# A fused attention block: a quarter's own maximum, its bias on ScalarE, fades once a stage, the division on GpSimd

## The chip, the cores and the metric

The kernel runs on one core of a Trainium2 chip. The metric is the device time of one execution in microseconds; the numbers shown are medians of several runs. A profile is one execution, recorded by the hardware profiler. The engines are called PE (TensorE), DVE (VectorE), ACT (ScalarE), POOL (GpSimd) and SP (SyncE). They run their own instruction streams in order and wait for each other by semaphores.

## The reference

The inputs are x (8 x 128 x 512) and a context (8 x 2048 x 384). Three blocks follow each other, each on a layer-normalised x and each added to it:

```python
# 1: cross attention, 8 heads of 64, every token of x against 2048 context rows
q = norm(x) @ Wq;  k = ctx @ Wk;  v = ctx @ Wv
x = x + softmax(q k^T / 8) v @ Wo + bo
# 2: causal attention in x, softmax over the query axis, divided by sqrt(512)
# 3: feed-forward 512 -> 2048 -> 512 with relu; hidden and weights rounded to fp8, the result to fp16
```

All time that matters here is in block 1. Products of float32 numbers are made in three passes over float16 halves (high x high, high x low, low x high), so each operand is split into a rounded copy (`_h`) and a remainder (`_l`).

## The kernel before, in words

A batch element b has four pairs of heads p; b and p together make a stage n (32 stages). Each stage has four quarters q of 512 context rows; a quarter of a stage is a slot s (128 slots). In slot s the engines work on different quarters at once:

- PE (`steady`, L478): `value_tiles(s)` fills v_ps with a share of v, `key_quarter(s)` fills k_ps with the keys of quarter s, `weighted_values(s - 5)` multiplies transposed probabilities by v into o_ps, `scores(s - 1)` makes the scores of the quarter before into e_ps (two buffers). v_ps and k_ps have one buffer each, so PE waits in slot s + 1 until DVE has made the low halves (`v_split`, L370; `k_split`, L387).
- ACT (L766): `v_high(s)` copies v_ps to float16; then for quarter x = s - 2 `fade_of(x)` (L712, not where q = 0) and `exps(x, 0)`: the exponential of the first head as float16 (p_h, L726) and again as float32 (p_f, L728); `k_high(s)` (L705); `exps(x, 1)` for the second head. Once a stage (q = 1) `ctx_high` rounds a quarter of the next context (L691), and once it starts a load.
- DVE (L994): `running_maximum(s - 2)` (L917), `accumulate(s - 6)` (L936), `v_low(s)` (L904), after the last quarter of a stage `o_norm` (L950), then `k_low(s)` (L911). In the last 16 slots a `split_weight` (L961) for the later blocks comes behind each slot.
- POOL (L1217): `p_low(s - 2)` takes p_h from p_f, giving the low half of the probabilities (L1205), and once a stage `ctx_low` does so for the context (L1197).
- SP (L317): transposes p_h and p_l by DMA.

The softmax is computed while the quarters go by. `running_maximum` reduces e_ps (with the sign turned, so it is a minimum that is kept), takes the minimum with the floor of the quarter before (L927), and makes the bias of the exponential from the new floor (L930). Where q > 0 it also takes the step from the old to the new floor (L933), from which ACT makes a fade factor; `accumulate` multiplies what has been summed by the fade and adds o_ps (L946). Where q = 0 there is no old floor, and acc is a copy (L941). `fade_of(x)` also waits for `acc_ready`, that is for the accumulate which DVE has in its stream behind the maximum of the same slot. `o_norm` takes the reciprocal of the sum of probabilities (a column of ones in v makes it), adds the two halves of the output and multiplies (L953 to L958).

The order of all streams is written out by hand; there is no planner. After slot 127 a drain of seven steps mixes the last quarters with the output projection (L596 to L600 on PE, L828 on ACT, L1106 on DVE, L1241 on POOL). At its start ACT waits for the last split weight and issues eight loads of x (L825 to L827). The second attention and the feed-forward follow. In it ACT alternates Identity with a bias (`q_or_k`, L806) with Exp (`prob_exp`, L813).

Of the kernel before, what the change touches and what calls it, by code (L numbers as in the profile page):

```python
# [4 lines left out]
F32 = mybir.dt.float32  # L5
# [20 lines left out]
VW = 2 * DH + 2  # L26
# [4 lines left out]
EXP_SCALE = DH ** -0.5 / (W_SCALE * W_SCALE)  # L31
SHIFT = 4.0
# [3 lines left out]
SLOTS = B * PAIRS * QUARTERS  # L36
# [19 lines left out]
def perceiver_kernel(nc, x, ctx_t, xwq, xwk, xwv, xwo, xbo, awq, abq, awk, abk, awv, abv,  # L56
# [9 lines left out]
        ("q_max", [P, 2, 1], F32), ("floor", [P, 2, 2, 1], F32), ("bias", [P, 2, 2, 1], F32), ("step", [P, 2, 2, 1], F32),  # L66
        ("fade", [P, 4, 2, 1], F32), ("acc", [P, 2, VW], F32), ("o_rec", [P, 2, 1], F32), ("o_sum", [P, 2, DH], F32),
# [52 lines left out]
    assert ffn2_end <= ctx1_base  # L120

    (o_all, ident, causal, bo_row, bv_row, b2_row, bq_col, bk_col, b1_col, b2_half, stats, mean_var, rstd, exponent,
     q_max, floor, bias, step, fade, acc, o_rec, o_sum) = keep.values()
# [22 lines left out]
    with ExitStack() as ctx:  # L146
# [48 lines left out]
        k_split = sem("k_split")  # L195
        e_filled = sem("e_filled")
        e_maxed = sem("e_maxed")
        floor_ready = sem("floor_ready")
        bias_ready = sem("bias_ready")
        step_ready = sem("step_ready")  # L200
        fade_ready = sem("fade_ready")
        p_hi = sem("p_hi")
        p_full = sem("p_full")
# [48 lines left out]
        out_stored = sem("out_stored")  # L252

        block = ctx.enter_context(nc.Block())

# [400 lines left out]
        def _(act):  # L656
# [55 lines left out]
            def fade_of(s):  # L712

                act.wait_ge(step_ready, s // QUARTERS * 3 + s % QUARTERS)
                if s >= QUARTERS:
                    act.wait_ge(acc_ready, s - 3)
                act.activation(fade[:, s % 4, :, :], step[:, s % 2, :, :], ACT.Exp, scale=EXP_SCALE).then_inc(fade_ready, 1)  # L717

            def exps(s, h):

                act.wait_ge(bias_ready, s + 1)
# [4 lines left out]
                act.activation(p_h[:, s % H_RING, h, :], e_ps[s % 2][:, h, :], ACT.Exp, scale=EXP_SCALE,  # L726
                               bias=bias[:, s % 2, h, :]).then_inc(p_hi, 1)
                act.activation(p_f[:, s % F_RING, h, :], e_ps[s % 2][:, h, :], ACT.Exp, scale=EXP_SCALE,  # L728
                               bias=bias[:, s % 2, h, :]).then_inc(p_full, 1)

            wq_high(0)
            wq_high(1)
# [32 lines left out]

            def steady(s):  # L766
                x = s - X_LAG
                if s < SLOTS:
                    v_high(s)
                if 0 <= x < SLOTS:  # L770
                    if x % QUARTERS:
                        fade_of(x)
                    exps(x, 0)
                if s < SLOTS:
                    k_high(s)
                if 0 <= x < SLOTS:
                    exps(x, 1)

            for s in range(SLOTS):
                n, q = stage_of(s)  # L780
# [81 lines left out]
        def _(dve):  # L862
# [54 lines left out]
            def running_maximum(s):  # L917

                q = s % QUARTERS
                dve.wait_ge(e_filled, s + 1)  # L920
                if q == 0:
                    dve.tensor_reduce(floor[:, s % 2, :, :], e_ps[s % 2][:, :, :], AX, ALU.max, negate=True)\  # L922
                        .then_inc(floor_ready, 1)
                else:
                    dve.tensor_reduce(q_max[:, :, :], e_ps[s % 2][:, :, :], AX, ALU.max, negate=True).then_inc(e_maxed, 1)  # L925
                    dve.wait_ge(e_maxed, s // QUARTERS * 3 + q)
                    dve.tensor_tensor(floor[:, s % 2, :, :], q_max[:, :, :], floor[:, (s - 1) % 2, :, :], ALU.min)\  # L927
                        .then_inc(floor_ready, 1)
                dve.wait_ge(floor_ready, s + 1)
                dve.tensor_scalar(bias[:, s % 2, :, :], floor[:, s % 2, :, :], EXP_SCALE, SHIFT, ALU.mult, ALU.add)\  # L930
                    .then_inc(bias_ready, 1)
                if q:
                    dve.tensor_tensor(step[:, s % 2, :, :], floor[:, s % 2, :, :], floor[:, (s - 1) % 2, :, :], ALU.subtract)\  # L933
                        .then_inc(step_ready, 1)

            def accumulate(s):  # L936

                q = s % QUARTERS
                dve.wait_ge(pv_done, s + 1)
                if q == 0:  # L940
                    ins = dve.tensor_copy(acc[:, :, :], o_ps[s % 2][:, 0:2 * VW].rearrange("p (h d) -> p h d", h=2))  # L941
                else:
                    dve.wait_ge(fade_ready, s // QUARTERS * 3 + q)
                    dve.wait_ge(acc_ready, s)
                    for h in range(2):
                        ins = dve.scalar_tensor_tensor(acc[:, h, :], acc[:, h, :], fade[:, s % 4, h, :],  # L946
                                                       o_ps[s % 2][:, h * VW:h * VW + VW], ALU.mult, ALU.add)
                ins.then_inc(acc_ready, 1)

            def o_norm(n):  # L950
                b, p = pair_of(n)
                dve.wait_ge(acc_ready, 4 * n + 4)
                dve.reciprocal(o_rec[:, :, :], acc[:, :, DH:DH + 1]).then_inc(o_rec_ready, 1)  # L953
                dve.tensor_tensor(o_sum[:, :, :], acc[:, :, 0:DH], acc[:, :, DH + 1:2 * DH + 1], ALU.add)\
                    .then_inc(o_sum_ready, 1)
                dve.wait_ge(o_rec_ready, n + 1)
                dve.wait_ge(o_sum_ready, n + 1)
                dve.tensor_tensor(o_all[:, b, p * P:p * P + P].rearrange("p (h d) -> p h d", h=2), o_sum[:, :, :],  # L958
                                  o_rec[:, :, :].broadcast_to([P, 2, DH]), ALU.mult).then_inc(o_ready, 1)

            def split_weight(i):  # L961
                k = weight_slot(i)
# [31 lines left out]
            def steady(s):  # L994

                done = s - PV_LAG - 1
                if 0 <= s - X_LAG < SLOTS:
                    running_maximum(s - X_LAG)
                if 0 <= done < SLOTS:
                    accumulate(done)  # L1000
                if s < SLOTS:
                    v_low(s)
                if 0 <= done < SLOTS and done % QUARTERS == 3:
                    o_norm(done // QUARTERS)
                if s < SLOTS:
                    k_low(s)

# [162 lines left out]
        def _(pool):  # L1170
# [46 lines left out]
            for s in range(SLOTS):  # L1217
                n, q = stage_of(s)
                if s >= X_LAG:
                    p_low(s - X_LAG)  # L1220
                if s < 2:
# [19 lines left out]
            for s in range(SLOTS, SLOTS + 6):  # L1241
                if s - X_LAG < SLOTS:
                    p_low(s - X_LAG)
                add_bias(s - SLOTS)
                if s > SLOTS + 1:
                    inverse_deviation(s - SLOTS - 2)
# [41 lines left out]
```

## Time and profile before

| | us |
|---|---|
| median of 3 runs | 1053.88 (1052.25 to 1054.06) |
| the profiled execution | 1052.84 |
| its span, first to last instruction | 1051.0 |
| PE busy | 971.7 (92%) |
| DVE busy | 755.9 (72%) |
| ACT busy | 558.6 (53%) |
| POOL busy | 418.1 (40%) |

The loop of 128 slots fills the span from about 50 to about 808 us; ahead of it x is normalised and q is made, behind it come the drain, the second attention and the feed-forward. A row of a timeline gives start, duration, engine, line, operation, the tile written and the tiles read, how many such instructions, and in brackets how long the engine was idle before and who released it. A duration begins when the engine takes up the instruction and ends with its last write, so neighbours on one engine can overlap a little, and an instruction that is held on its way is simply long. PE's ends are modelled, so starts are the safer numbers there.

### The profile page before, as it was taken

How to read it: one execution, taken by the hardware profiler on the slowest of the kernel's cores; microseconds unless marked ns; L12 is line 12 of the kernel's file. 1: busy time of each engine (PE TensorE's matmuls, PEld its weight loads, DVE VectorE, ACT ScalarE, POOL GpSimd, SP SyncE). 2: the span in 40 equal slices, each digit the busy share in tenths (PEclk: the TensorE clock that was granted, in tenths of full speed). 3: DMA queues.
4: the chain of work that ended last, by engine and by line, in shares of the span. 5: the costliest groups of instructions: out<-in, count | busy, mean ns of one | idle time of the engine just before them, and what ended most of it. 6: DMA issues, size and time to landing. Idle time of an engine off the chain costs nothing.

```text
span 1051.0 us, 19633 instructions
## 1 busy us (share of the span) xinstructions
PE 971.7 (92%) x7469; PEld 577.6 (55%) x7472; DVE 755.9 (72%) x1344; ACT 558.6 (53%) x1007; POOL 418.1 (40%) x227
## 2 busy tenths in 40 slices
PE   4889999999999999999999999999887889999998
PEld 2456656665565656565555666565554444554443
DVE  6467787878778787878788778778877763574533
ACT  3366666666666666666666666665554321222220
POOL 3155455545444455545454455444333650110000
PEclk9899999999999999999999999999999899999999
DMA  7146665667657666678656666668565701003302
GB/s 270 61 131 121 121 122 121 121 122 145 123 116 121 120 121 121 121 127 140 126 120 120 117 121 123 121 105 152 122 126 117 130 1 41 1 31 90 91 31 80
DMA packets 295789, 115.86 MB, mean 110 GB/s; under 512 B 272529, under 2 KB 272529, under 8 KB 295697
## 3 DMA queue, kind: packets, MB, share of 16 engines
q1 hardware_dynamic: 281264, 86.82, 46.0%
q10 hardware_dynamic: 14432, 27.79, 8.8%
q8 instruction: 61, 1.00, 0.4%
q14 instruction: 32, 0.25, 0.1%
HBM read 45.36 MB, written 2.10 MB: 45 GB/s over the span
## 4 chain that ended last, share of the span: by engine, by line
DVE 51%; PE 21%; ACT 16%; issue 8%; ACTq 2%; DMA 1%; POOL 1%; SPq 0%; POOLq 0%; DVEq 0%
PE e_ps L362 14%; DVE floor L927 13%; DVE q_max L925 10%; DVE k_l L915 8%; ACT p_f L728 7%; ACT k_h L710 6%; DVE bias L930 5%; DVE acc L946 5%; DVE floor L922 3%; PE o_ps L593 3%; DVE step L933 1%; PE v_ps L362 1%; ACT p_h L726 1%; PE k_ps L362 1%; ACTq L755 1%
## 5 line engine op out<-in xcount | busy, mean ns | idle before, releaser
L1205 POOL TENSOR_TENSOR p_l<-p_f,p_h 128x1024 f16<-128x1024 f32 x128 | 279.0, 2180 | 395.5 <-ACT p_f L728 387.8
L915 DVE TENSOR_TENSOR k_l<-k_ps,k_h 128x512 f16<-128x512 f32 x128 | 88.5, 692 | 142.1 <-ACT k_h L710 142.1
L726 ACT ACTIVATE p_h<-e_ps,bias 128x512 f16<-128x512 f32 x256 | 177.2, 692 | 20.0 <-DVE bias L930 19.8
L728 ACT ACTIVATE p_f<-e_ps,bias 128x512 f32<-128x512 f32 x256 | 177.5, 694 | 0.0
L362 PE MATMUL v_ps<-wv_h,ctx_h 128*128 128x256 f16 x768 | 125.7, 272 | 44.2 <-DVE v L907 38.9
L717 ACT ACTIVATE fade<-step 128x2 f32<-128x2 f32 x96 | 19.5, 203 | 241.4 <-DVE acc L946 232.9
L927 DVE TENSOR_TENSOR floor<-q_max,floor 128x2 f32<-128x2 f32 x96 | 134.1, 1397 | 3.3
L362 PEld LDWEIGHTS v_ps<-wv_h,ctx_h 128*128 128x128 f16 x768 | 66.3, 97 | 109.3 <-issue 101.2
L362 PE MATMUL v_ps<-wv_l,ctx_h 128*128 128x256 f16 x768 | 126.0, 273 | 0.0
L362 PE MATMUL v_ps<-wv_h,ctx_l 128*128 128x256 f16 x768 | 126.0, 273 | 0.0
L925 DVE TENSOR_REDUCE q_max<-e_ps 128x2 f32<-128x1024 f32 x96 | 116.6, 1215 | 0.0
L1197 POOL TENSOR_TENSOR ctx_l<-raw,ctx_h 128x1536 f16<-128x1536 f32 x32 | 99.3, 3104 | 29.1 <-ACT ctx_h L691 29.1
L423 PE MATMUL o_ps<-v,pt_h 128*128 128x130 f16 x1024 | 106.2, 220 | 3.0 <-DVE acc L946 1.6
L362 PE MATMUL k_ps<-ctx_h,wk_h 128*128 128x512 f16 x384 | 104.2, 380 | 0.5 <-DVE k_l L915 0.5
L362 PE MATMUL k_ps<-ctx_h,wk_l 128*128 128x512 f16 x384 | 103.9, 379 | 0.0
L362 PE MATMUL k_ps<-ctx_l,wk_h 128*128 128x512 f16 x384 | 103.8, 379 | 0.0
L426 PE MATMUL o_ps<-v,pt_l 128*128 128x65 f16 x1024 | 102.7, 192 | 0.0
L423 PEld LDWEIGHTS o_ps<-v,pt_h 128*128 128x128 f16 x1024 | 91.8, 97 | 19.3 <-issue 4.6
L426 PEld LDWEIGHTS o_ps<-v,pt_l 128*128 128x128 f16 x1024 | 90.4, 98 | 14.6
L907 DVE TENSOR_TENSOR v<-v_ps,v 128x512 f16<-128x512 f32 x128 | 87.5, 684 | 6.8 <-ACT v L702 6.8
L702 ACT ACTIVATE v<-v_ps 128x512 f16<-128x512 f32 x128 | 78.9, 616 | 15.0 <-PE v_ps L362 14.8
L362 PEld LDWEIGHTS v_ps<-wv_l,ctx_h 128*128 128x128 f16 x768 | 75.3, 98 | 8.9
(153 smaller groups left out, 1404.8 us busy)
## 6 DMA issues: line engine op xcount, KB each, us to landing
raw<-in_ctx_t ACTq DMA_DIRECT2D x26, 768.0 KB, 4.8
w_raw<-in_w_t SPq DMA_DIRECT2D x32, 256.0 KB, 2.8
raw<-in_ctx_t SPq DMA_DIRECT2D x6, 768.0 KB, 4.6
pt_h<-p_h SPq DMA_TRANSPOSE x128, 3.5
pt_l<-p_l SPq DMA_TRANSPOSE x128, 3.1
xr<-in_x ACTq DMA_DIRECT2D x8, 256.0 KB, 5.2
out<-xr SPq DMA_DIRECT2D x8, 256.0 KB, 2.0
x_in<-in_x SPq DMA_DIRECT2D x4, 256.0 KB, 5.1
```

The costliest lines, as they stand in the source:

```text
L362: mm = pe.matmul(acc, a(c), m(c), start=(i == 0), stop=(i == len(todo) - 1))
L423: pe.matmul(acc_bank[:, h * VW:h * VW + VW], pt_h[:, s % T_RING, h * JT + j, :], v[g][:, tile, 2 * (p % 2) + h, :], start=(j == 0 and h == ...
L426: mm = pe.matmul(acc_bank[:, h * VW:h * VW + DH + 1], pt_l[:, s % T_RING, h * JT + j, :], v[g][:, tile, 2 * (p % 2) + h, 0:DH + 1], start= ...
L702: act.activation(v[g][:, j0:j0 + 2, :, 0:DH], v_ps[:, :].rearrange("p (j h d) -> p j h d", j=2, d=DH), ACT.Copy).then_inc(v_hi, 1)
L726: act.activation(p_h[:, s % H_RING, h, :], e_ps[s % 2][:, h, :], ACT.Exp, scale=EXP_SCALE, bias=bias[:, s % 2, h, :]).then_inc(p_hi, 1)
L728: act.activation(p_f[:, s % F_RING, h, :], e_ps[s % 2][:, h, :], ACT.Exp, scale=EXP_SCALE, bias=bias[:, s % 2, h, :]).then_inc(p_full, 1)
L907: dve.tensor_tensor(v[g][:, j0:j0 + 2, :, DH + 1:2 * DH + 1], v_ps[:, :].rearrange("p (j h d) -> p j h d", j=2, d=DH), v[g][:, j0:j0 + 2, ...
L915: dve.tensor_tensor(k_l[:, n % 2, cols], k_ps[:, :], k_h[:, n % 2, cols], ALU.subtract).then_inc(k_split, 1)
L925: dve.tensor_reduce(q_max[:, :, :], e_ps[s % 2][:, :, :], AX, ALU.max, negate=True).then_inc(e_maxed, 1)
L927: dve.tensor_tensor(floor[:, s % 2, :, :], q_max[:, :, :], floor[:, (s - 1) % 2, :, :], ALU.min)\
L1197: pool.tensor_tensor(ctx_l[b % 2][:, q, :, :], raw[:, i % 2, :, :], ctx_h[b % 2][:, q, :, :], ALU.subtract).then_inc(ctx_split, 1)
L1205: pool.tensor_tensor(p_l[:, s % L_RING, :, :], p_f[:, s % F_RING, :, :], p_h[:, s % H_RING, :, :], ALU.subtract).then_inc(p_split, 1)
```

## The change

- DVE keeps only the reduction in each quarter (`quarter_maximum`); there is no running floor. Its result q_max has two buffers.
- ACT makes the bias of the quarter, from the quarter's own maximum (`quarter_bias`, an Identity with scale and bias), as its first work in a slot, ahead of `v_high(s)`.
- When a stage has all its four biases, DVE takes their minimum (`stage_low`, behind `v_low` in the slot of its last maximum), and ACT makes four fades for each of the two heads in two operations (`fade_of(n)`, behind the last exponentials of the stage).
- `accumulate` multiplies each quarter's o_ps by that quarter's fade and adds what is there, two operations in every quarter; acc has two buffers, one for a stage.
- `o_norm` moves to POOL, behind `p_low`, but for its reciprocal, which DVE does behind the accumulate (`o_reciprocal`). It also stands in POOL's drain, ahead of `add_bias`.

```diff
+            def quarter_bias(s):
+                n, q = stage_of(s)
+                act.wait_ge(e_maxed, s + 1)
+                act.activation(bias[:, n % 2, :, q], q_max[:, s % 2, :], ACT.Identity, scale=EXP_SCALE, bias=SHIFT)\
+                    .then_inc(bias_ready, 1)
+            def fade_of(n):
+                act.wait_ge(low_ready, n + 1)
+                if n >= 2:
+                    act.wait_ge(acc_ready, 4 * n - 4)
+                for h in range(2):
+                    ins = act.activation(fade[:, n % 2, h, :], bias[:, n % 2, h, :], ACT.Exp, scale=-1.0, bias=low[:, n % 2, h, :])
+                ins.then_inc(fade_ready, 1)
...
             def steady(s):
                 x = s - X_LAG
+                if 0 <= x < SLOTS:
+                    quarter_bias(x)
                 if s < SLOTS:
                     v_high(s)
                 if 0 <= x < SLOTS:
-                    if x % QUARTERS:
-                        fade_of(x)
                     exps(x, 0)
                 if s < SLOTS:
                     k_high(s)
                 if 0 <= x < SLOTS:
                     exps(x, 1)
+                    if x % QUARTERS == 3:
+                        fade_of(x // QUARTERS)
...
+            def quarter_maximum(s):
+                dve.wait_ge(e_filled, s + 1)
+                dve.tensor_reduce(q_max[:, s % 2, :], e_ps[s % 2][:, :, :], AX, ALU.max, negate=True).then_inc(e_maxed, 1)
+            def stage_low(n):
+                dve.wait_ge(bias_ready, 4 * n + 4)
+                dve.tensor_reduce(low[:, n % 2, :, :], bias[:, n % 2, :, :], AX, ALU.min).then_inc(low_ready, 1)
             def accumulate(s):
...
                 dve.wait_ge(pv_done, s + 1)
                 if q == 0:
-                    ins = dve.tensor_copy(acc[:, :, :], o_ps[s % 2][:, 0:2 * VW].rearrange("p (h d) -> p h d", h=2))
+                    dve.wait_ge(fade_ready, n + 1)
+                    if n >= 2:
+                        dve.wait_ge(o_ready, n - 1)
...
+                for h in range(2):
+                    new, total, faded = o_ps[s % 2][:, h * VW:h * VW + VW], acc[:, n % 2, h, :], fade[:, n % 2, h, q:q + 1]
+                    if q == 0:
+                        ins = dve.tensor_scalar(total, new, faded, None, ALU.mult)
+                    else:
+                        ins = dve.scalar_tensor_tensor(total, new, faded, total, ALU.mult, ALU.add)
                 ins.then_inc(acc_ready, 1)
-            def o_norm(n):
+            def o_reciprocal(n):
                 dve.wait_ge(acc_ready, 4 * n + 4)
+                if n:
+                    dve.wait_ge(o_ready, n)
+                dve.reciprocal(o_rec[:, :, :], acc[:, n % 2, :, DH:DH + 1]).then_inc(o_rec_ready, 1)
...
+            def o_norm(n):
+                b, p = pair_of(n)
+                pool.wait_ge(o_rec_ready, n + 1)
+                pool.tensor_tensor(o_sum[:, :, :], acc[:, n % 2, :, 0:DH], acc[:, n % 2, :, DH + 1:2 * DH + 1], ALU.add)\
+                    .then_inc(o_sum_ready, 1)
+                pool.wait_ge(o_sum_ready, n + 1)
+                pool.tensor_tensor(o_all[:, b, p * P:p * P + P].rearrange("p (h d) -> p h d", h=2), o_sum[:, :, :],
+                                   o_rec[:, :, :].broadcast_to([P, 2, DH]), ALU.mult).then_inc(o_ready, 1)
```

## Rows read from the trace of the kernel before

**Rows 1.** The page of the profile, its first line.
```profile
span 1051.0 us, 19633 instructions
```

**Rows 2.** Busy time by stretch: PE, PEld, DVE, ACT, POOL, clock, DMA.
```profile
300.00:400.00 100.00, 95.37 (x837) 60.06 (x833) 80.00 (x137) 64.96 (x119) 50.61 (x22) 1.00 0.68 122
...
950.00:1000.00 50.00, 50.00 (x234) 22.66 (x232) 27.49 (x63) 13.39 (x20) 0.00 (x0) 1.00 0.30 90
```

**Rows 3.** Waits, 200 to 700 us: total us, times, longest.
```profile
ACT fade L717 <- DVE acc L946: 156.4, 63, 2.9
...
PE v_ps L362 <- DVE v L907: 21.1, 43, 0.6
```

**Rows 4.** Timeline of one slot with q > 0.
```profile
400.67 0.60 ACT L710 ACTIVATE k_h<-k_ps 128x512 f16<-128x512 f32 x1
...
401.30 0.69 DVE L915 TENSOR_TENSOR k_l<-k_ps,k_h 128x512 f16<-128x512 f32 x1 [1.39 <-ACT k_h L710]
...
401.91 1.21 DVE L925 TENSOR_REDUCE q_max<-e_ps 128x2 f32<-128x1024 f32 x1
...
402.50 2.13 POOL L1205 TENSOR_TENSOR p_l<-p_f,p_h 128x1024 f16<-128x1024 f32 x1 [3.99 <-ACT p_f L728]
...
403.16 1.49 DVE L927 TENSOR_TENSOR floor<-q_max,floor 128x2 f32<-128x2 f32 x1
...
404.83 0.61 DVE L946 SCALAR_TENSOR_TENSOR acc<-acc,fade,o_ps 128x130 f32<-128x130 f32 x2
...
405.35 0.69 DVE L907 TENSOR_TENSOR v<-v_ps,v 128x512 f16<-128x512 f32 x1
405.53 0.20 ACT L717 ACTIVATE fade<-step 128x2 f32<-128x2 f32 x1 [2.62 <-DVE acc L946]
405.64 0.69 ACT L726 ACTIVATE p_h<-e_ps,bias 128x512 f16<-128x512 f32 x1
...
406.18 0.49 PE L362 MATMUL v_ps<-wv_h,ctx_h 128*128 128x256 f16 x3 [0.49 <-DVE v L907]
```

**Rows 5.** Timeline of a slot with q = 0, POOL and DVE.
```profile
414.75 2.14 POOL L1205 TENSOR_TENSOR p_l<-p_f,p_h 128x1024 f16<-128x1024 f32 x1 [3.99 <-ACT p_f L728]
416.84 3.10 POOL L1197 TENSOR_TENSOR ctx_l<-raw,ctx_h 128x1536 f16<-128x1536 f32 x1
...
415.40 1.50 DVE L930 TENSOR_SCALAR bias<-floor 128x2 f32<-128x2 f32 x1
...
417.16 0.68 DVE L907 TENSOR_TENSOR v<-v_ps,v 128x512 f16<-128x512 f32 x1
```

**Rows 6.** Timeline of PE: v of slots 6, 8 and 127, k of slot 6.
```profile
82.86 0.50 PE L362 MATMUL v_ps<-wv_h,ctx_h 128*128 128x256 f16 x3
...
84.83 0.81 PE L362 MATMUL k_ps<-ctx_h,wk_h 128*128 128x512 f16 x3
...
93.78 0.50 PE L362 MATMUL v_ps<-wv_h,ctx_h 128*128 128x256 f16 x3
...
800.55 0.49 PE L362 MATMUL v_ps<-wv_h,ctx_h 128*128 128x256 f16 x3 [0.45 <-DVE v L907]
```

**Rows 7.** Groups of instructions: busy us, mean ns, then idle before.
```profile
L691 ACT ACTIVATE ctx_h<-raw 128x1536 f16<-128x1536 f32 x32 | 48.1, 1503 | 3.9 <-DMA raw<-in_ctx_t 3.9
...
L662 ACT ACT_TABLE_LOAD x1 | 1.3, 1283 | 2.6 <-issue 2.6
...
L1228 POOL TENSOR_TENSOR xr<-xr,bo_row 128x512 f32<-128x512 f32 x8 | 10.2, 1280 | 0.0
```

**Rows 8.** Timeline at the end of the loop.
```profile
807.83 0.69 DVE L915 TENSOR_TENSOR k_l<-k_ps,k_h 128x512 f16<-128x512 f32 x1 [1.39 <-ACT k_h L710]
...
808.43 0.42 DVE L966 TENSOR_SCALAR av_h<-raw 128x512 f16<-128x512 f32 x1
...
809.61 4.41 ACTq L827 DMA_DIRECT2D xr<-in_x  x8
```

More of the change, by code:

```diff
@@ L65, in perceiver_kernel @@
         ("stats", [P, B, 6], F32), ("mean_var", [P, B, 2], F32), ("rstd", [P, B], F32), ("exponent", [P, B], F32),
-        ("q_max", [P, 2, 1], F32), ("floor", [P, 2, 2, 1], F32), ("bias", [P, 2, 2, 1], F32), ("step", [P, 2, 2, 1], F32),
-        ("fade", [P, 4, 2, 1], F32), ("acc", [P, 2, VW], F32), ("o_rec", [P, 2, 1], F32), ("o_sum", [P, 2, DH], F32),
+        ("q_max", [P, 2, 2], F32), ("bias", [P, 2, 2, QUARTERS], F32), ("low", [P, 2, 2, 1], F32),
+        ("fade", [P, 2, 2, QUARTERS], F32), ("acc", [P, 2, 2, VW], F32), ("o_rec", [P, 2, 1], F32), ("o_sum", [P, 2, DH], F32),
     ])
@@ L122, in perceiver_kernel @@
     (o_all, ident, causal, bo_row, bv_row, b2_row, bq_col, bk_col, b1_col, b2_half, stats, mean_var, rstd, exponent,
-     q_max, floor, bias, step, fade, acc, o_rec, o_sum) = keep.values()
+     q_max, bias, low, fade, acc, o_rec, o_sum) = keep.values()
     q_h, q_l = queries.values()
@@ L197, in perceiver_kernel @@
         e_maxed = sem("e_maxed")
-        floor_ready = sem("floor_ready")
         bias_ready = sem("bias_ready")
-        step_ready = sem("step_ready")
+        low_ready = sem("low_ready")
         fade_ready = sem("fade_ready")
@@ L710, in k_high @@
                 act.activation(k_h[:, n % 2, q * QW:q * QW + QW], k_ps[:, :], ACT.Copy).then_inc(k_hi, 1)
[L712 to L717, printed above, removed]
+            def quarter_bias(s):
[10 more added lines that the diff above has]
+                ins.then_inc(fade_ready, 1)
             def exps(s, h):
+                n, q = stage_of(s)
                 act.wait_ge(bias_ready, s + 1)
@@ L726, in exps @@
                 act.activation(p_h[:, s % H_RING, h, :], e_ps[s % 2][:, h, :], ACT.Exp, scale=EXP_SCALE,
-                               bias=bias[:, s % 2, h, :]).then_inc(p_hi, 1)
+                               bias=bias[:, n % 2, h, q:q + 1]).then_inc(p_hi, 1)
                 act.activation(p_f[:, s % F_RING, h, :], e_ps[s % 2][:, h, :], ACT.Exp, scale=EXP_SCALE,
-                               bias=bias[:, s % 2, h, :]).then_inc(p_full, 1)
+                               bias=bias[:, n % 2, h, q:q + 1]).then_inc(p_full, 1)
             wq_high(0)
@@ L915, in k_low @@
                 dve.tensor_tensor(k_l[:, n % 2, cols], k_ps[:, :], k_h[:, n % 2, cols], ALU.subtract).then_inc(k_split, 1)
-            def running_maximum(s):
-                q = s % QUARTERS
+            def quarter_maximum(s):
                 dve.wait_ge(e_filled, s + 1)
[L921 to L934, printed above, removed]
@@ L942, in accumulate @@
                 else:
-                    dve.wait_ge(fade_ready, s // QUARTERS * 3 + q)
                     dve.wait_ge(acc_ready, s)
-                    for h in range(2):
-                        ins = dve.scalar_tensor_tensor(acc[:, h, :], acc[:, h, :], fade[:, s % 4, h, :],
-                                                       o_ps[s % 2][:, h * VW:h * VW + VW], ALU.mult, ALU.add)
+                for h in range(2):
[4 more added lines that the diff above has]
+                        ins = dve.scalar_tensor_tensor(total, new, faded, total, ALU.mult, ALU.add)
@@ L948, in accumulate @@
                 ins.then_inc(acc_ready, 1)
-            def o_norm(n):
-                b, p = pair_of(n)
+            def o_reciprocal(n):
                 dve.wait_ge(acc_ready, 4 * n + 4)
[L953 to L959, printed above, removed]
+                if n:
+                    dve.wait_ge(o_ready, n)
+                dve.reciprocal(o_rec[:, :, :], acc[:, n % 2, :, DH:DH + 1]).then_inc(o_rec_ready, 1)
@@ L997, in steady @@
                 if 0 <= s - X_LAG < SLOTS:
-                    running_maximum(s - X_LAG)
+                    quarter_maximum(s - X_LAG)
                 if 0 <= done < SLOTS:
                     accumulate(done)
+                    if done % QUARTERS == 3:
+                        o_reciprocal(done // QUARTERS)
                 if s < SLOTS:
                     v_low(s)
-                if 0 <= done < SLOTS and done % QUARTERS == 3:
-                    o_norm(done // QUARTERS)
+                if 0 <= s - X_LAG < SLOTS and (s - X_LAG) % QUARTERS == 3:
+                    stage_low((s - X_LAG) // QUARTERS)
                 if s < SLOTS:
@@ L1220, in _ @@
                     p_low(s - X_LAG)
+                done = s - PV_LAG - 1
+                if done >= 0 and done % QUARTERS == 3:
+                    o_norm(done // QUARTERS)
                 if s < 2:
@@ L1243, in _ @@
                     p_low(s - X_LAG)
+                done = s - PV_LAG - 1
+                if done % QUARTERS == 3:
+                    o_norm(done // QUARTERS)
                 add_bias(s - SLOTS)
```

2 lines of the change are left out of this document (1 added, 1 removed).

## The prediction

> **What bounds the kernel now.** I read the busy shares by stretch first, then the waits of the long middle stretch, then the timeline of one slot (a slot is one step s of the steady loop: one quarter of the keys for one pair of heads), and last the start and the end of the loop.
>
> The profiled execution took 1052.84 us, its span is 1051.0 us [rows 1], so 1.84 us lie around it; the median of the runs is 1053.88 us, 1.0 more than this execution. In the middle PE is busy 95.4 of 100 us at a granted clock of 1.00, DVE 80.0, ACT 65.0 [rows 2]. That looks like a kernel bound by TensorE with little to gain. The waits say otherwise: PE waits for the low half of v (DVE L907), ACT's fade waits for DVE's accumulate (156.4 us in 63 waits) [rows 3], and POOL waits for ACT's exponentials (3.99 us ahead of 402.50 [rows 4]). Three engines that wait for each other in turn are a loop, and the timeline shows it [rows 4]. Beginning at the fade (405.53), with the same places of the slot before read 6.12 us earlier where only that slot is shown: 0.11 us to the first exponential (405.64); 1.15 us of two exponentials, to k_h at 400.67 + 6.12 = 406.79; k_h and the other two exponentials until POOL can start p_l, 1.83 (400.67 to 402.50); then p_l, 2.13, at whose end (404.63) the DVE's little floor operation ends too (403.16 + 1.49 = 404.65); 0.2 to the accumulate (404.83) with bias and step between; 0.7 from there to the fade (405.53). The sum is 6.12 us, and that is the period.
>
> The striking row is the floor operation, 1.49 us for 2 elements a partition. It has no work for that: it ends with POOL's operation. The slots with q = 0 show the same with another operation: there the bias (415.40, 1.50 us) ends at 416.90 and POOL's p_l at 414.75 + 2.14 = 416.89, while a v_l with an input in PSUM runs its usual 0.68 us inside POOL's ctx_l [rows 5]. So small DVE operations that touch SBUF alone are held until POOL is done, and those with an operand in PSUM are not. The Trainium skill, "GPSIMD Engine Reference", Specifications, states that the engine shares its SBUF interfaces with VectorE and contends with a DVE instruction in a two-port mode or with two SBUF inputs. By that rule the floor and bias operations are held and the reduction from PSUM is not; the trace agrees (1.49 and 1.50 us against 1.25 us from one reduction to the next operation).
>
> What would TensorE need alone? At the start of the loop there are slots in which it never waits: v begins at 82.86 and at 93.78, two slots later, so 5.46 us a slot with all four of its jobs in it [rows 6]. From 93.78 (slot 8) to 800.55 (slot 127) there are 119 slots in 706.77 us, 5.94 each [rows 6]. The difference, 0.48 us a slot, is what can be had.
>
> **The change part by part.**
>
> *Floor, bias and step leave DVE.* In each slot DVE now has the reduction, the accumulate, v_l and k_l. What goes is 403.16 to 404.83 = 1.67 us a slot [rows 4], and what goes with it is the hold by POOL and therefore the loop. What is late next? I lay out the new slot from the start of v on PE, 0. v is filled at 2.0 (82.86 to 84.83 [rows 6]) and k, with as many columns, at 4.0. The scores of the quarter before were finished just ahead of 0, so the reduction runs 0.15 to 1.4 (401.91 to 403.16 [rows 4]), the accumulate to 2.0. ACT's bias starts at 1.4 and costs 0.11 (below); v_h then waits for PE only, 2.1 to 2.7; v_l to 3.4. PE needs v_l at 5.46: 2 us to spare. The first two exponentials end at 3.9, k_h starts at 4.1, k_l runs 4.7 to 5.4, and PE needs it at 5.46 + 2.0 = 7.5. The other two exponentials end at 5.9, p_l on POOL at 8.0, far ahead of its use. So in this layout PE is last everywhere.
>
> The loops that remain do not hold it either. The tightest goes k_h, k_l, reduction, bias, v_h, two exponentials, k_h: 0.63 + 0.61 + 1.25 + 0.11 + 0.6 (v_h taken like k_h) + 1.16 = 4.36 us [rows 4]. In one slot of four ACT also has the context's high half, 1.5 us [rows 7], and the two fades, between the exponentials and the next bias; that loop is on ACT alone, and in k_h, two exponentials, fades, ctx_h, bias, v_h, two exponentials it is 1.6 (k_h and two exponentials, from the 1.83 above less the hop to POOL) + 0.2 + 1.5 + 0.11 + 0.6 + 1.16 = 5.2 us, still under 5.46. In the last 16 slots DVE splits a weight between k_l and the reduction, about 1.1 us (808.43 to ACT's release near 809.5 [rows 8]); that loop is 5.45, even with PE. I give these slots 0 to 0.1 more, 0 to 1.6 us in all, and take 0.5.
>
> *The bias on ACT.* One operation a slot, 128 x 2, ahead of v_h. The nearest row is the fade, of the same size on the same engine, which holds the next instruction back by 0.11 us (405.53 to 405.64 [rows 4]). It takes the fade's place in three slots of four. Its wait is new: behind it on ACT stand v_h and the exponentials, and PE waits for v_h's sequel. By the layout the wait ends 0.6 us before v_h could start. Cost: between 0 and 0.11 x 128 = 14 us, if it were on the path; I take 0 in the loop because of those 0.6 us and 0.1 at the start of the loop, where ACT is the late one.
>
> *Fades once a stage.* Two ACT operations and one DVE reduction over 4 elements a stage against three and no reduction. Both ACT operations stand after the exponentials, ahead of the accumulate that wants them by some 0.7 us. If DVE's reduction of low is held by POOL it costs at most 2.13 us x 32, of which v_l's 2 us of room takes all but 0.1; I take 0.
>
> *The accumulate.* Twice 128 x 130 from PSUM in every quarter where q = 0 had one copy; 0.1 us more in one slot of four, hidden. Could POOL now hold the accumulate, since it comes at once after the reduction and has acc in SBUF? Below, it isn't held; above, it starts at p_l's end at about 2.5, and v_l at 3.1 still has its room. Cost 0 by both.
>
> *The division on GpSimd.* A reciprocal stays on DVE; two 128 x 128 operations go to POOL. Between 0 and 1.28 us each, the time of POOL's 128 x 512 [rows 7]; I take 0.4 each. POOL's stage is then 4 x 2.13 + 3.10 + 0.8 = 12.4 of 21.8 us, 14.2 by the upper bound. Behind it in POOL's queue are ctx_l, wanted many slots later, and p_l, wanted two slots later: hidden, 0.
>
> *The sum.* 119 slots x 0.48 = 57.0 us. The end of the loop: v of slot 127 starts at 800.55, its k_l at 807.83, that is 7.3 later; the last split frees ACT's loads at 809.61, 9.1 later [rows 6, 8]. In the new order k_l starts at about 4.7 and the loads go out at about 6.6 with the 16-slot loop's lag: 2.4 us gained. Behind that the drain keeps its waits; the last quarter's bias no longer stands behind two accumulates, and GpSimd has the last division, so between -1 and +2 us, taken as 0.5 gained. Added: 0.1 at the start and 0.5 in the last 16 slots. 1051.0 - 57.0 - 2.4 - 0.5 + 0.6 = 991.7; with 1.84 around it 993.5, and a median 1.0 above: 994.5, say 994. Everything before slot 8 and after the drain stays.
>
> **The rivals.**
>
> *A new loop at ScalarE.* The bias now stands ahead of v_h, and it waits for a reduction; ACT's slot with the context and fades is 5.2 already. If lags that I do not see lengthen the loops to 5.65, the gain falls by 0.19 x 119 = 23 us, to 1017. For: three engines again wait in turn, and the 16-slot loop has no room. Against: 1.1 us of room in the usual slot. Its time: 1005 to 1030.
>
> *It does not do what it says.* The hold passes to another DVE operation or PE finds another wait, and the period stays 5.94: 1053. For: the accumulate touches SBUF. Against: ACT no longer waits for anything behind the accumulate but the fades of a stage, and slots 6 and 7 ran at 5.46 already.
>
> *Slower: ScalarE changes tables.* Identity stands between Exp and Copy in every slot. If each change loaded a table, at 1.28 us [rows 7], twice a slot, the 4.36 loop becomes 6.9 and the kernel 119 x (6.9 - 5.94) = 114 us slower, 1168. It decides from 1.6 us a slot on. Against: the whole trace has one load [rows 7], though Identity (L806) and Exp (L813) already alternate in the second attention. The Trainium skill, "ScalarE: Activation LUTs", Table sets: the hidden batching unit, has the cheap functions, identity among them, in every set; by that rule no load is added, and the single load in the trace agrees. The page prices a switch at 2.66 us with its drain; as an estimate from that, two a slot would make the loss 119 x (4.36 + 5.32 - 5.94) = 445 us.
>
> Would a denser PE be granted less clock? At 950 to 1000 us it is busy 50 of 50 us at 1.00 [rows 2]; I leave this in the slower share.
>
> **How the numbers follow.** Forecast 0.75, with its own range 985 to 1005 (5.40 to 5.55 us a slot, 7 us down and 11 up). ScalarE loop 0.15. No change 0.03, within 0.2%, which is about what a measurement of this kernel can tell. Slower 0.04, and 0.03 for a gain of which most is lost, 1030 to 1050. Faster is then 0.93, same 0.03, slower 0.04. For eight in ten the range is 985 to 1016: most of the forecast's side and the lower half of the ScalarE loop's.
>
> **What would show it.** v on PE every 5.46 us, PE over 99% busy in the middle, no DVE operation of 2 elements above 0.2 us in most slots, ACT's bias ended by the reduction and not ending PE's waits, POOL's division under 1 us a stage. Wrong would be: a period above 5.6, a PE wait for v_l or k_l in the middle, more than one table load, a granted clock under 1.00.

## The result and the profile after

The changed kernel takes 993.21 us (median of 4 runs, 992.35 to 994.40) against 1053.93 beside it: a ratio of 0.9428, 95% interval 0.9412 to 0.9444. The forecast was 994 in a range of 985 to 1016. The span of the profiled execution went from 1051.0 to 991.6 us, 59.4 less.

The page of the changed kernel: the span, then busy time and share of the engines.

```profile
span 991.6 us, 19444 instructions
PE 952.3 (96%) x7472; PEld 582.3 (59%) x7472; DVE 570.1 (57%) x1024; ACT 588.8 (59%) x1103; POOL 440.7 (44%) x291
```

DVE has lost 186 us of busy time, POOL and ACT have gained 23 and 30, and PE does the same work in fewer microseconds. The stretches that answer to [rows 2], in the same columns:

```profile
300.00:400.00 100.00, 100.00 (x900) 65.33 (x897) 58.69 (x100) 75.81 (x144) 57.55 (x34) 1.00 0.65 129
94.00:710.00 616.00, 616.00 (x5528) 403.14 (x5527) 366.35 (x637) 458.75 (x872) 342.73 (x195) 1.00 0.67 135
```

PE is busy 616 of 616 us at a granted clock of 1.00. The waits from 200 to 700 us (total, times, longest) answer to [rows 3]:

```profile
POOL p_l L1209 <- ACT p_f L738: 215.2, 69, 3.3
...
DVE v L919 <- ACT v L702: 78.5, 90, 1.0
ACT bias L716 <- DVE q_max L932: 72.1, 70, 1.8
...
ACT v L702 <- PE v_ps L362: 37.9, 63, 0.6
ACT k_h L710 <- PE k_ps L362: 16.4, 86, 0.2
```

No line of the list is a wait of PE for DVE any more. Every engine waits for another, and the last in each chain is PE: v_h and k_h begin when PE has filled their bank. Read with the timeline of a slot with its bias at 400.51, against [rows 4]:

```profile
399.26 1.23 DVE L932 TENSOR_REDUCE q_max<-e_ps 128x2 f32<-128x1024 f32 x1
399.63 2.13 POOL L1209 TENSOR_TENSOR p_l<-p_f,p_h 128x1024 f16<-128x1024 f32 x1 [2.82 <-ACT p_f L738]
...
400.40 0.60 DVE L954 SCALAR_TENSOR_TENSOR acc<-o_ps,fade,acc 128x130 f32<-128x130 f32 x2
...
400.51 0.20 ACT L716 ACTIVATE bias<-q_max 128x2 f32<-128x2 f32 x1 [0.96 <-DVE q_max L932]
...
401.32 0.60 ACT L702 ACTIVATE v<-v_ps 128x512 f16<-128x512 f32 x1 [0.60 <-PE v_ps L362]
...
401.95 0.69 DVE L919 TENSOR_TENSOR v<-v_ps,v 128x512 f16<-128x512 f32 x1 [0.95 <-ACT v L702]
...
403.26 0.60 ACT L710 ACTIVATE k_h<-k_ps 128x512 f16<-128x512 f32 x1 [0.19 <-PE k_ps L362]
...
403.89 0.69 DVE L927 TENSOR_TENSOR k_l<-k_ps,k_h 128x512 f16<-128x512 f32 x1 [1.25 <-ACT k_h L710]
...
404.61 0.50 PE L362 MATMUL v_ps<-wv_h,ctx_h 128*128 128x256 f16 x3
...
405.09 2.13 POOL L1209 TENSOR_TENSOR p_l<-p_f,p_h 128x1024 f16<-128x1024 f32 x1 [3.34 <-ACT p_f L738]
...
406.50 0.17 DVE L961 RECIPROCAL o_rec<-acc 128x2 f32<-128x2 f32 x1
...
410.07 0.50 PE L362 MATMUL v_ps<-wv_h,ctx_h 128*128 128x256 f16 x3
410.18 1.22 DVE L932 TENSOR_REDUCE q_max<-e_ps 128x2 f32<-128x1024 f32 x1
410.36 0.49 ACT L725 ACTIVATE fade<-bias,low 128x4 f32<-128x4 f32 x2
...
411.32 0.60 DVE L952 TENSOR_SCALAR acc<-o_ps,fade 128x130 f32<-128x130 f32 x2
```

POOL runs p_l over the reduction as before, and now over the accumulate too, and neither is held: the accumulate starts 1.14 us behind the reduction's start, while p_l is still under way. v_l ends at 402.64, and PE wants it at 404.61, so it has the 2 us of room that the layout gave it. v starts on PE every 5.46 us. Slots 8 and 127 on PE, as in [rows 6]:

```profile
93.20 0.50 PE L362 MATMUL v_ps<-wv_h,ctx_h 128*128 128x256 f16 x3
...
743.34 0.50 PE L362 MATMUL v_ps<-wv_h,ctx_h 128*128 128x256 f16 x3
```

That is 650.14 us for 119 slots, 5.463 each.

### The profile page after: what moved, and what is told of

Same layout as the page of the kernel before. It is cut to its first block, busy times and chain, and to the rows that moved or that the text cites. A ratio compares the mean times of both kernels' runs of the same rounds, so it can differ in the third digit from the quotient of the medians.

```text
span 991.6 us, 19444 instructions
## 1 busy us (share of the span) xinstructions
PE 952.3 (96%) x7472; PEld 582.3 (59%) x7472; DVE 570.1 (57%) x1024; ACT 588.8 (59%) x1103; POOL 440.7 (44%) x291
## 4 chain that ended last, share of the span: by engine, by line
PE 89%; DVE 4%; POOL 2%; DMA 1%; ACT 1%; issue 1%; ACTq 0%; SPq 0%; POOLq 0%; DVEq 0%
PE v_ps L362 27%; PE k_ps L362 25%; PE e_ps L362 14%; PE e_ps L403 9%; PE o_ps L423 6%; PE o_ps L426 3%; PE o_ps L593 3%; DMA wq_raw<-in_xwq 1%; PE v_ps L566 1%; DVE stats L1028 0%; DVE x_in L886 0%; ACTq L839 0%; DMA raw<-in_ctx_t 0%; PE k_ps L514 0%; POOL rstd L1191 0%
## 5 line engine op out<-in xcount | busy, mean ns | idle before, releaser
L736 ACT ACTIVATE p_h<-e_ps,bias 128x512 f16<-128x512 f32 x256 | 174.4, 681 | 0.1
L932 DVE TENSOR_REDUCE q_max<-e_ps 128x2 f32<-128x1024 f32 x128 | 156.5, 1223 | 14.4
L702 ACT ACTIVATE v<-v_ps 128x512 f16<-128x512 f32 x128 | 76.2, 595 | 51.8 <-PE v_ps L362 51.5
L716 ACT ACTIVATE bias<-q_max 128x2 f32<-128x2 f32 x128 | 26.3, 205 | 112.6 <-DVE q_max L932 107.0
L710 ACT ACTIVATE k_h<-k_ps 128x512 f16<-128x512 f32 x128 | 76.4, 597 | 24.7 <-PE k_ps L362 23.6
```

What stands on the lines that cost most here:

```text
L932: dve.tensor_reduce(q_max[:, s % 2, :], e_ps[s % 2][:, :, :], AX, ALU.max, negate=True).then_inc(e_maxed, 1)
```

## Where the 59.4 us are

Each figure is a stretch of before less the same stretch of after, so the sum is the difference of the spans.

| stretch | before | after | gained | forecast |
|---|---|---|---|---|
| start to v of slot 8 | 93.78 | 93.20 | 0.6 | -0.1 |
| v of slot 8 to v of slot 127 | 706.77 | 650.14 | 56.6 | 56.5 |
| v of slot 127 to ACT's loads of x | 9.06 | 6.52 | 2.5 | 2.4 |
| the loads to the end | 241.39 | 241.74 | -0.3 | 0.5 |

The start's 0.6 can't be put down to the change: executions of one kernel differ by as much there. In a second trace of the changed kernel, taken later, v of slot 8 starts at 93.86 and not at 93.20. The last row differs too: it is 239.3 us in that second trace, a gain of 2.1 and not a loss of 0.3. The two rows of the loop are the same in both traces to 0.01 us.

## The experiments

Two questions were open though the number was right. Is the loop of four engines the cause, or just that DVE has less to do? And which of the change's parts earn the gain? The twelve runs came in three groups; each is compared with the kernel before on its own chip, at 1052.5 to 1053.9. A gain of 2 or 3 us over the changed kernel is given as a difference of medians, and but for the third group the changed kernel was not run beside them; by the ratios these gains are 0.5 to 0.8 us smaller.

**One line moved in the kernel before.** ACT makes the fade behind the first two exponentials.

```diff
                 if 0 <= x < SLOTS:
-                    if x % QUARTERS:
-                        fade_of(x)
                     exps(x, 0)
+                    if x % QUARTERS:
+                        fade_of(x)
```

> The kernel before with one thing moved: ACT makes the fade behind the first two exponentials of a quarter and not ahead of them, so the exponentials no longer stand behind DVE's accumulate. All of DVE's work and POOL's hold stay. Theory of the loop (fade, exponentials, p_l on POOL, held floor operation, accumulate, fade = 6.12 us): accumulate leaves the loop, which is then 1.15 + 1.83 + 2.13 + 0.15 = 5.3 us, under PE's 5.46, so most of the gain comes: 995 to 1002, with 16 slower slots at the end where a weight is split. Rival, that DVE's amount of work or the small operations themselves are what costs: DVE does exactly what it did, so 1050 to 1054.

Measured: 998.34 us, ratio 0.9487 (0.9471 to 0.9503). All of DVE's and POOL's work is the same, and 55 of the 61 us are gained. The timeline of one slot in the order of time, DVE and ACT, and two PE rows from the last 16 slots:

```profile
400.34 1.26 DVE L927 TENSOR_TENSOR floor<-q_max,floor 128x2 f32<-128x2 f32 x1
401.64 0.17 DVE L930 TENSOR_SCALAR bias<-floor 128x2 f32<-128x2 f32 x1
...
401.79 0.60 DVE L946 SCALAR_TENSOR_TENSOR acc<-acc,fade,o_ps 128x130 f32<-128x130 f32 x2
```
```profile
401.84 0.69 ACT L726 ACTIVATE p_h<-e_ps,bias 128x512 f16<-128x512 f32 x1
...
403.00 0.20 ACT L717 ACTIVATE fade<-step 128x2 f32<-128x2 f32 x1
```
```profile
735.00 0.49 PE L362 MATMUL v_ps<-wv_h,ctx_h 128*128 128x256 f16 x3 [0.35 <-DVE v L907]
...
740.88 0.49 PE L362 MATMUL v_ps<-wv_h,ctx_h 128*128 128x256 f16 x3 [0.35 <-DVE v L907]
```

The floor operation is still held, 1.26 us, but the exponentials begin at 401.84, together with the accumulate and not behind it. In the middle PE's period is 5.46 us. What is missing against the changed kernel is at the end of the loop, where the loop with a split weight is longer than PE's: v at 735.00 and 740.88, 5.88 apart.

**The other half of the loop: no hold.** The kernel before, with the fade where it was, and POOL's p_l made to wait for DVE's small operations of the next quarter.

```diff
                 pool.wait_ge(p_hi, 2 * s + 2)
+                after = s + 1
+                if after < SLOTS:
+                    if after % QUARTERS:
+                        pool.wait_ge(step_ready, after // QUARTERS * 3 + after % QUARTERS)
+                    else:
+                        pool.wait_ge(bias_ready, after + 1)
```

> The kernel before with one wait added on POOL: p_l of a quarter starts only when DVE has made the step (where q = 0, the bias) of the next quarter, so POOL is idle when DVE does its small operations and can hold none. All of DVE's work and the fade behind the accumulate stay as before. Theory: the hold is the other half of the loop; without it floor, bias and step take 0.3 us together and the loop k_h, k_l, reduction, small operations, accumulate, fade, two exponentials is 4.8 us, under 5.46: floor near 0.15 to 0.2 us, 994 to 1000 in all. Rival, that the first small operation behind a reduction is slow whatever POOL does: 1050 and above, since POOL now starts even later.

Measured: 996.50 us, ratio 0.9457 (0.9444 to 0.9470). A wait was added and nothing taken away, and the kernel is 5.4% faster. One slot, DVE and POOL:

```profile
399.37 1.23 DVE L925 TENSOR_REDUCE q_max<-e_ps 128x2 f32<-128x1024 f32 x1
400.63 0.16 DVE L927 TENSOR_TENSOR floor<-q_max,floor 128x2 f32<-128x2 f32 x1
```
```profile
401.29 2.13 POOL L1211 TENSOR_TENSOR p_l<-p_f,p_h 128x1024 f16<-128x1024 f32 x1 [3.34 <-DVE step L933]
```

The same floor operation, first behind the same reduction, takes 0.16 us when POOL is idle and 1.49 when it is not. So both halves are shown: to open the loop at either place is enough, for then it is shorter than PE's 5.46. The 3.3 us that are missing against the changed kernel are again at the end of the loop: between v of slot 8 and ACT's loads of x the trace has 3.4 us more.

**p_l in two operations.** The kernel before, POOL subtracting one head at a time.

```diff
-                pool.tensor_tensor(p_l[:, s % L_RING, :, :], p_f[:, s % F_RING, :, :], p_h[:, s % H_RING, :, :],
-                                   ALU.subtract).then_inc(p_split, 1)
+                for h in range(2):
+                    ins = pool.tensor_tensor(p_l[:, s % L_RING, h, :], p_f[:, s % F_RING, h, :], p_h[:, s % H_RING, h, :],
+                                             ALU.subtract)
+                ins.then_inc(p_split, 1)
```

> The kernel before, with POOL's p_l made in two operations of 128x512 and not one of 128x1024, same elements. Theory of the hold (a small SBUF operation on DVE waits until POOL's instruction ends): the floor operation is let in between the two, near 1 us earlier, so the loop is 6.12 - 1.0 = 5.1, under 5.46, and the time 995 to 1005; the floor operation lasts about 0.5 us. Rival, that the floor operation is slow by itself behind a reduction (1.49 us whatever POOL does): 1052 to 1056, with POOL a little longer.

Measured: 1052.82 us, ratio 1.0001 (0.9991 to 1.0012). The time was forecast wrong and the floor operation right, and the trace has both. DVE and POOL in one slot:

```profile
401.38 0.52 DVE L927 TENSOR_TENSOR floor<-q_max,floor 128x2 f32<-128x2 f32 x1
401.93 1.08 DVE L930 TENSOR_SCALAR bias<-floor 128x2 f32<-128x2 f32 x1
```
```profile
400.72 2.27 POOL L1206 TENSOR_TENSOR p_l<-p_f,p_h 128x512 f16<-128x512 f32 x2 [3.80 <-ACT p_f L728]
```

The floor operation is let in at POOL's change of instructions and ends at 401.90. But DVE has a second operation of the kind, the bias, and POOL's second half is under way: it is held to 403.01, with POOL's end at 402.99. A hold goes by instruction. I had counted the first operation alone; the exponentials wait for the second.

**The bias on DVE again.** The changed kernel, the bias made by a tensor_scalar behind the reduction.

```diff
-                act.wait_ge(e_maxed, s + 1)
-                act.activation(bias[:, n % 2, :, q], q_max[:, s % 2, :], ACT.Identity, scale=EXP_SCALE, bias=SHIFT)\
-                    .then_inc(bias_ready, 1)
...
+                dve.wait_ge(e_maxed, s + 1)
+                dve.tensor_scalar(bias[:, n % 2, :, q], q_max[:, s % 2, :], EXP_SCALE, SHIFT, ALU.mult, ALU.add)\
+                    .then_inc(bias_ready, 1)
```

> The changed kernel with the bias made by DVE (a tensor_scalar of 128x2 in SBUF behind the reduction) instead of ScalarE. Theory: POOL holds it again to the end of p_l, some 2.6 us into the slot, which leaves the exponentials, 2.7 to 3.9, just ahead of k_h at 4.1; PE stays the bound in 112 slots, and the 16 slots with a split weight take about 5.7: 993 to 1000. Rival, that moving the bias to ScalarE is what brings the gain: most of it is lost, 1030 or more.

Measured: 995.55 us, ratio 0.9456 (0.9442 to 0.9470). The bias is held again, 1.39 us in the mean and up to 1.8, and it costs 2 to 3 us in all (by the median and by the ratio; the intervals just overlap). The trace has 2.1 us more at the end of the loop, where v's starts are up to 5.77 us apart. The place of the bias is not what brings the gain.

**A held operation that nobody waits for.** The changed kernel with a minimum of q_max with itself behind each reduction.

```diff
+                dve.wait_ge(e_maxed, s + 1)
+                dve.tensor_tensor(idle[:, :], q_max[:, s % 2, :], q_max[:, s % 2, :], ALU.min)
```

> The changed kernel with one more DVE operation in each quarter, a minimum of q_max with itself (2 elements, both inputs in SBUF) behind the reduction, whose result nobody reads. Theory: POOL holds it to the end of p_l as it held the floor operation, 0.9 to 1.5 us long, but ScalarE's bias no longer stands behind it and v_l has 2 us of room, so the hold costs nothing: 992 to 996, the most in the last 16 slots. Rival, that the hold as such costs wherever it stands: 0.5 us or more a slot, 1040 and above.

Measured: 993.53 us, ratio 0.9443 (0.9428 to 0.9458). The group of these operations, busy us and mean ns:

```profile
L934 DVE TENSOR_TENSOR idle<-q_max 128x2 f32<-128x2 f32 x128 | 170.4, 1331 | 4.4
```

DVE is busy for 170 us more, nearly all of it held, and the kernel is no slower than its own spread.

**The reduction twice.** The changed kernel with 1.14 us more of real DVE work ahead of the bias.

```diff
+                dve.tensor_reduce(idle[:, :], e_ps[s % 2][:, :, :], AX, ALU.max, negate=True)
                 dve.tensor_reduce(q_max[:, s % 2, :], e_ps[s % 2][:, :, :], AX, ALU.max, negate=True).then_inc(e_maxed, 1)
```

> The changed kernel with the reduction done twice in each quarter, the first time into a tile that nobody reads: 1.14 us more of DVE work a slot, ahead of the bias. My loop k_h, k_l, reduction, bias, v_h, two exponentials is 4.3 us and becomes 5.4, just under PE's 5.46; in the last 16 slots, with a weight split in it, it goes from 5.3 to 6.4, 1.0 over. So nothing in the first 112 slots and 15 to 18 us at the end: 1008 to 1014. Rival, that DVE's idle time (43%) hides it everywhere: 993 to 996. Rival, that DVE has no room anywhere: 1.1 us in all 128 slots, 1130 and above.

Measured: 1009.43 us, ratio 0.9596 (0.9579 to 0.9614), in the range worked out from the loop and outside both rivals. v on PE in the middle, and in the last 16 slots:

```profile
646.46 0.50 PE L362 MATMUL v_ps<-wv_h,ctx_h 128*128 128x256 f16 x3
...
651.92 0.50 PE L362 MATMUL v_ps<-wv_h,ctx_h 128*128 128x256 f16 x3
```
```profile
737.50 0.49 PE L362 MATMUL v_ps<-wv_h,ctx_h 128*128 128x256 f16 x3 [0.90 <-DVE v L919]
...
743.92 0.49 PE L362 MATMUL v_ps<-wv_h,ctx_h 128*128 128x256 f16 x3 [0.90 <-DVE v L919]
```

5.46 us still in the middle and 6.42 at the end, where 6.4 was worked out. The loop had 1.1 us of room in the usual slot and next to none in the last sixteen.

**The division on DVE again.** The changed kernel, with the two operations of `o_norm` on DVE behind v_l; measured twice, the second time beside the changed kernel.

```diff
                 if s < SLOTS:
                     v_low(s)
+                if 0 <= done < SLOTS and done % QUARTERS == 3:
+                    o_norm(done // QUARTERS)
...
                     p_low(s - X_LAG)
-                done = s - PV_LAG - 1
-                if done >= 0 and done % QUARTERS == 3:
-                    o_norm(done // QUARTERS)
```

> The changed kernel with the two 128x128 operations of the division on DVE again, behind v_l. Theory: v_l and k_l have 2 us of room, so the loop stays at 5.46 a slot; 992 to 995. Rival, that the division's place matters (0.6 us or a hold of up to 2 us once a stage, 32 stages): 1010 or more.

> The changed kernel with the division on DVE, once more beside the changed kernel. The two traces agree to 0.1 us up to the drain and part there: with the division on GpSimd the inverse deviations behind it come later, DVE's norm waits for them and is then held, PE's wait is longer and its clock falls. Theory: 2 to 3 us faster than the changed kernel, 990 to 991. Rival, that it was the chip or chance: the same within 1 us.

> The changed kernel once more, beside the next two on the same chip: 993.

Measured: 990.65 us, ratio 0.9411 (0.9397 to 0.9425), then 990.29, 0.9405 (0.9387 to 0.9422), with the changed kernel at 992.82, 0.9424 (0.9409 to 0.9439). Both times 2.5 us faster by the medians, about 2 by the ratios, and the intervals still overlap. From v of slot 8 to v of slot 127 all four traces take 650.1 us, so the division's place in the loop is worth nothing. What the traces show of the difference is in the drain. The changed kernel, DVE's norm and then PE's transposes:

```profile
781.39 1.49 DVE L1035 TENSOR_SCALAR o_all<-xr,mean_var,rstd 128x512 f32<-128x512 f32 x1 [0.94 <-POOL rstd L1191]
```
```profile
785.87 0.63 PE L514 MATMUL k_ps<-ident,o_all 128*128 128x128 f32 x4 [1.30 <-DVE at_l L1022]
...
789.57 1.91 PE L362 MATMUL e_ps<-wo_h,ot_h 128*128 128x512 f16 x4
```
```profile
785.00:795.00 10.00, 7.19 (x32) 3.76 (x33) 5.57 (x11) 2.37 (x4) 1.76 (x4) 0.83 0.01 2
```

With the division on DVE (the second run), the same two places:

```profile
780.58 0.51 DVE L1046 TENSOR_SCALAR o_all<-xr,mean_var,rstd 128x512 f32<-128x512 f32 x1
```
```profile
784.09 0.63 PE L514 MATMUL k_ps<-ident,o_all 128*128 128x128 f32 x4 [0.78 <-DVE at_l L1033]
```

On POOL the division stands ahead of an addition and an inverse deviation; DVE's norm waits 0.94 us for that and is then held by POOL's next addition, 1.49 us against 0.51. PE waits 0.5 us longer. From the norm's start to the transposes it is 4.48 us in both traces of the changed kernel and 3.51 in both with the division on DVE: this 1.0 us is shown.

Behind PE's waits four matmuls took 1.91 us where others take 1.03: the granted clock from 785 to 795 us was 0.83, the mark of a stretch at the lower of its two levels (1.2 and 2.4 GHz). The second trace of the changed kernel has the longer wait and no such stretch. From the transposes to the end that trace and both with the division on DVE take 204.1 us, the first one 205.7, so the stretch costs 1.7 us where it comes. The other runs give a hint that the longer wait brings it more often. Of the seven traces with a wait of 1.3 us ahead of these transposes, one had a granted clock of 1.00 in the ten us behind them, three 0.83 and three 0.66 (206.7 to 207.1 us to the end); of the seven with a wait of 0.8, three had 1.00, four 0.83 and none 0.66. These are single executions of different kernels, so how much of the 2.5 us is the clock stays open.

**The loads of x later.** The changed kernel, with the eight loads that ACT issues at the drain's start (4.82 us) put behind the exponentials and copies of its first four steps.

```diff
-            act.wait_ge(wx_split, 16)
-            for r in range(B):
-                act.dma_start(xr[:, r, :], x[r]).then_inc(xr_landed[r], 16)
             for s in range(SLOTS, SLOTS + 6):
                 steady(s)
...
+                if s == SLOTS:
+                    act.wait_ge(wx_split, 16)
+                if s < SLOTS + 4:
+                    for r in (2 * (s - SLOTS), 2 * (s - SLOTS) + 1):
+                        act.dma_start(xr[:, r, :], x[r]).then_inc(xr_landed[r], 16)
```

> The changed kernel with the eight loads of x that ScalarE issues at the start of the drain (4.8 us) put behind the exponentials and copies of the drain's first four steps, two a step. Theory: the exponentials of slot 126 begin 3.7 us earlier and PE, which stands idle there for 6.3 us, takes up its transposes earlier by about as much: 989 to 991. Rival, that the loads come late for the additions on POOL and the residual on DVE: 993 to 996.

Measured: 990.21 us, ratio 0.9406 (0.9389 to 0.9423), as expected: PE waits 2.5 us there and no longer 6.3.

**A context quarter later.** In the changed kernel ACT waits in slot 1 for a load that is not wanted before slot 16. Both halves of that work go to slot 2, on ACT and on POOL.

```diff
-                if q == 1 and QUARTERS + n < B * QUARTERS:
+                if q == (1 if n else 2) and QUARTERS + n < B * QUARTERS:
                     ctx_high(QUARTERS + n)
```

> The changed kernel with the fifth context quarter rounded (ScalarE) and subtracted (GpSimd) at the end of slot 2 and not of slot 1. In slot 1 ScalarE waits 3.8 us for its load, and v_h of slot 2 stands behind it, so PE is idle 3.3 us and then runs 6.4 us for a slot of 4.8, most of it at the lower clock. Theory: both go, 4 to 5 us: 988 to 990. Rival, that the wait only moves to slot 3: 992 to 994.

Measured: 990.88 us, ratio 0.9413 (0.9396 to 0.9430), 2.3 us faster where 4 to 5 were expected. v of slots 2, 3 and 4 on PE:

```profile
58.51 0.50 PE L362 MATMUL v_ps<-wv_h,ctx_h 128*128 128x256 f16 x3
...
63.28 0.50 PE L362 MATMUL v_ps<-wv_h,ctx_h 128*128 128x256 f16 x3
...
68.04 0.50 PE L362 MATMUL v_ps<-wv_h,ctx_h 128*128 128x256 f16 x3
```

PE's wait and its slow slot are gone: 9.5 us from slot 2 to slot 4, where the changed kernel has 14.5 (57.54 to 72.04). Of these 5 us, 1.0 is missing again ahead of slot 2, where executions differ by as much, and 1.5 behind the loop: the ten us behind the drain's transposes have a granted clock of 0.66 in this trace, and from there to the end it takes 1.2 us longer than the changed kernel. So the start gives what was expected, and the shortfall is elsewhere.

**The three together.**

> The changed kernel with three of the tried changes together: the division on DVE (2.6 us), the loads of x behind the first exponentials of the drain (3.0), the fifth context quarter a slot later (2.3 to 5). If they add up 983 to 986; if the first two overlap in the drain 985 to 988.

Measured: 985.35 us, ratio 0.9359 (0.9342 to 0.9376): faster than both kernels, 7.5 us below the changed kernel on the same chip (7.9 if the single gains added up). The two ranges that were written down overlap at 985 to 986, so it does not say whether the gains in the drain add up or overlap.

## Why the prediction was right, point by point

*The bound.* The loop was the right reading, and the two experiments on the kernel before show each of its halves by itself. PE's own slot, taken from two slots at the start in which it never waits, was 5.46 and is 5.463. The 6.12 us that the prediction calls the period is that of two slots in four; the other two take 5.6 to 5.7, so a stage of four took 23.5 us. The sum used the mean over 119 slots, 5.94, so nothing hangs on it.

*The reading of the hold* was too wide. I wrote that small DVE operations which touch SBUF alone are held. The reciprocal touches SBUF alone, and in the changed kernel it runs its 0.17 us at 406.50, inside POOL's 405.09 to 407.22. What was held is an operation with two tensors in SBUF (floor, and o_sum, which took 1.40 us beside p_l in the run with the added wait and 0.28 where POOL was idle) and a tensor_scalar in SBUF (bias, norm). The rule of the Trainium skill that the prediction cites there ("GPSIMD Engine Reference", Specifications) is narrower than my reading, two SBUF inputs or a two-port mode, and the reciprocal, with one input, agrees with it. The bias has one tensor input as well, so it falls under that rule only if it ran in such a mode, which no trace shows. The wide reading cost the number nothing.

*The loops that remain.* 4.36 us was forecast and about 4.3 is right (v_h holds ACT for 0.49, not 0.6); with a split weight 5.45 against 5.3, by the reduction done twice. The 0.5 us that I added for the last 16 slots was not needed.

*The bias on ACT* costs nothing in the loop: it stands in ACT's wait, 0.8 us ahead of v_h. *The fades* end 0.5 us ahead of the accumulate that wants them, where I had 0.7.

*The division* is the term that was mis-sized. Its two operations take 0.41 and 0.40 us, as taken, and are hidden in the loop. In the drain I gave the whole of the change 0.5 us of gain within -1 to +2. In the traces compared above it is 0.3 us of loss: 0.6 gained up to DVE's norm and 1.0 lost from there to the transposes. By the two comparisons of medians the division costs 2.5 in all, of which the traces show this 1.0. What I had left out is what stands behind it on POOL: the inverse deviation for which DVE's norm waits, and the hold on that norm.

*The rivals.* A loop at ScalarE would have shown in a period above 5.6. The changed kernel has 5.46 to the last slot; above 5.6 came only at the end of the loop in two of its variants, 5.77 with the bias on DVE and 6.42 with the reduction doubled. Table changes: the operations are there without them. The clock was 1.00 over all 616 us of a PE without a gap.

*Luck.* The loop's 56.6 us against 56.5 is no luck: every trace of the changed kernel and of the variants that leave its loop alone has 650.1 us there. That the whole sum, 993.5, meets the profiled execution, 993.46, is partly luck: the start gave 0.7 more than forecast and the drain 0.8 less, and another execution of the same kernel took 991.65. The 1.0 us added from the profiled execution to the median was wrong, for the median lies 0.25 below it. And the forecast's own range should have begun at 987, not 985, by the 7 us that it names.

## What to carry to other kernels

A high busy share of the largest engine does not say that it is the bound: look for the period of the loop, and for a stretch in which that engine never waits; the difference is what can be had. When engines wait for each other in turn, write the loop down as a sum of starts to starts; the cheapest link to cut may be an instruction's place in one stream, which here gave nine tenths of what a rewrite of the softmax gave. Work moved to an idle engine is free only where nothing behind it in that engine's queue is waited for: look at the drain as well as the loop.

## What the runs showed of the hardware

GpSimd's hold on VectorE goes by whole instructions on both sides: an operation of 2 elements took 0.16 us alone, 0.52 with 0.5 us of GpSimd's instruction left and 1.49 with 1.5 left, and the next of its kind was held anew. The reduction, the accumulate and v_l, each with an operand in PSUM, and a reciprocal with one operand in SBUF were not held.

It also goes the other way. In the last 16 slots p_l starts 0.14 us behind DVE's second operation of the weight split, which has two operands in SBUF, and it takes 2.54 us there and 2.13 elsewhere. The changed kernel, slot 126:

```profile
738.22 0.69 DVE L970 SCALAR_TENSOR_TENSOR av_l<-raw,av_h 128x512 f16<-128x512 f32 x1
738.36 2.54 POOL L1209 TENSOR_TENSOR p_l<-p_f,p_h 128x1024 f16<-128x1024 f32 x1 [2.92 <-ACT p_f L738]
```

The whole 0.41 us that p_l is longer fits into what was left of DVE's operation, 0.55 us. The same two rows stand in the kernel before (808.88 and 809.03).

GpSimd's subtraction of 128x1024 split into two of 128x512 took 2.27 us in place of 2.13, so a second instruction cost 0.14.
